# Attention and ternary feed-forward on one core: rows of x loaded interleaved, a step's queries turned by one transfer

## The chip, the cores and the metric

One core of one Trainium2 chip. The metric is device time of one launch in microseconds. The kernel before took 1701.72 us (median of 3 runs, 1698.91 to 1708.31). Engines are named as in the profile: PE (TensorE; PEld is its weight load), DVE (VectorE), ACT (ScalarE), POOL (GpSimd), SP (SyncE, which here only issues DMAs).

## The reference

```python
x = L0_attn_x                                   # [4, 1024, 512] f32
xn = layernorm(x)
c_Q  = rms_norm(xn @ Wq_down, q_norm_w)         # 512 -> 192
q_nop, q_pe = c_Q @ Wq_up, c_Q @ Wq_pe          # 16 heads x 128, 16 heads x 64
c_KV = rms_norm(xn @ Wkv_down, kv_norm_w)       # 512 -> 128
k_nop, v = split(c_KV @ Wkv_up)                 # 8 key/value heads x 128
k_pe = rms_norm(xn @ Wk_pe, k_pe_norm_w)        # one rotary key of 64 for all heads
q = concat(q_nop, rope(q_pe)); k = concat(k_nop, rope(k_pe))
attn = softmax(causal(q @ k.T * 192 ** -0.5))
y = (attn @ v) @ Wo
ffn = ternary(xn) @ (ternary(weight) + rram_variation).T
out = x + y + ffn
```

## The kernel before

**Latent form.** The prologue folds the key and value up-projections into the query and output weights, so that all 16 heads share one key matrix (128 latent numbers and 64 rotary ones a token, the rotary part held twice) and one value matrix of 128 numbers. Each fp32 number is held as a high and a low fp16 part, and a product is three matmuls (high by high, high by low, low by high).

**Tiles and steps.** A tile is 128 rows of x: 4 batches of 8 tiles, 32 in all, in the order of `ORDER`. The first three tiles of a batch are laid between the wide ones of the batch before. A tile has four steps, one for each group of four heads, so 128 steps `n`. Tile i of a batch sees i + 1 key blocks. A step has four score rows-of-128 `u = 4n + h`. With `a, g = divmod(h, 2)`, one of them holds 64 queries (side `a` of the tile) of two heads (pair `g`): the side with the first 64 queries needs 64 key columns fewer (`columns`).

**Queries.** PE makes a step's queries in PSUM with rows of x on the partitions (`up`, `up_pe`), ACT and DVE write high and low parts to `QS`, [128 rows, 1536]. SP then turns them by DMA (`turn_queries` in `sync_attention`, L1823 to L1832): two transfers, one for partitions 0 to 63 and one for 64 to 127, each to 12 blocks of 64 columns of `Q`. So a side's two heads lie next to each other, and `query_weights` (L413) takes 128 neighbouring columns as the stationary operand of the score matmuls (L672 to L676, L692 to L705), whose moving operand is the key matrix `K`.

**Softmax.** DVE adds the mask and takes the row's extreme (L1485), ACT the exponential and its sum (L1082), POOL scales the sum (L1719), DVE takes the reciprocal (L1493), ACT and DVE write the scaled high and low parts to `F` (L1077, L1499). SP turns `F` to `FT` by DMA (L1848).

**Values and output.** PE multiplies `V` (stationary) by `FT` (moving) into one PSUM bank of 512 columns (`weighed`, L724; matmuls L737 to L739, for the diagonal block of most steps L748 to L760 on halves, in the last step L774 to L776). The bank's columns are (head, side, query in the side), with the 64 queries of a side next to each other. ACT and DVE split the bank to `YH` and `YL`, and `combine` (L779) multiplies them as stationary operands by the output weights.

**Per tile.** `keep` (L1768) turns the tile's latents (`C`) and keys (`K`, L1784) by DMA and copies the values (`V`, L1786). The keys go straight to the tile's 128 columns of `K`.

**Order.** Each engine's program is written out by hand in one loop over steps. Scores of step n + 2 stand beside the values of step n on PE (`AHEAD = 2`), queries are made four steps ahead. SP's queue holds, a step, the turning of queries of step n + 3 and that of `F` of step n + 2, and once a tile `turn_x` and `keep`, all in program order.

Of the kernel before, what the change touches and what calls it, by code (L numbers as in the profile page):

```python
# [15 lines left out]
T = NB * NT  # L16
# [168 lines left out]
def rows(dram, t):  # L185

    b, i = ORDER[t]
    return dram[b, i * 128:i * 128 + 128, :]

# [13 lines left out]
class Memory:  # L203


    def __init__(self, ctx, nc):
# [37 lines left out]
        self.FT = own("FT", [128, RING * 1024], F16)  # L244
        self.Q = own("Q", [128, 2, 2, 768], F16)
        self.QS = own("QS", [128, 2, 1536], F16)
# [78 lines left out]
class Sems:  # L325


    def __init__(self, ctx, nc):
# [10 lines left out]
        self.ld_x, self.st_o, self.xt_in = sems("ld_x", XSLOTS), sem("st_o"), sem("xt_in")  # L339
        self.c_in, self.k_in, self.v_in = sem("c_in"), sem("k_in"), sem("v_in")  # L340
        self.const, self.wqs, self.nwq = sem("const"), sem("wqs"), sem("nwq")
# [18 lines left out]
        self.qh, self.ql, self.ph, self.pl = sem("qh"), sem("ql"), sem("ph"), sem("pl")  # L360
        self.q_in = [sems("q_first", 2), sems("q_second", 2)]
        self.s, self.mk, self.ex, self.sm, self.rc, self.fh, self.fl = (
# [50 lines left out]
def query_weights(m, n, h):  # L413


    a, g = divmod(h, 2)
    Q = m.Q[:, n % 2, a, :]
    return [Q[:, 256 * x + 128 * g:256 * x + 128 * g + 128] for x in range(3)]

# [225 lines left out]
def tensor_attention(e, m, s, tiles, queries):  # L645
# [12 lines left out]
    def score(n, h):  # L658
        b, i, g = where(n)
        u = 4 * n + h  # L660
        off, cuts = score_cuts(u)
        base = key_slot(b, 0) * 128
        qh, ql, qp = query_weights(m, n, h)
        e.wait_ge(s.q_in[h // 2][n % 2], 16 * (n // 2 + 1))
        e.wait_ge(s.k_in, 16 * (n // NG + 1))
        if u >= 2:
            e.wait_ge(s.mk, u - 1)
        else:
            e.wait_ge(s.wfl, 4)
        for lo, hi in cuts:  # L670
            o, keys = m.pS[u % 2][:, off + lo:off + hi], slice(base + lo, base + hi)
            e.eng.matmul(o, qh, m.K[:, AHI, keys], start=True, stop=False)  # L672
            e.eng.matmul(o, qh, m.K[:, ALO, keys], start=False, stop=False)
            e.eng.matmul(o, ql, m.K[:, AHI, keys], start=False, stop=False)
            e.eng.matmul(o, qp, m.K[:, BHI, keys], start=False, stop=False)
            op = e.eng.matmul(o, qp, m.K[:, BLO, keys], start=False, stop=True)  # L676
        op.then_inc(s.s, 1)

    def pair(n, p):
# [3 lines left out]
        base, K = key_slot(b, 0) * 128, m.K  # L683
        e.wait_ge(s.q_in[p][n % 2], 16 * (n // 2 + 1))
        e.wait_ge(s.k_in, 16 * (n // NG + 1))
        for h in (2 * p, 2 * p + 1):
# [24 lines left out]
    def weigh_ready(n):  # L711

        for z in range(GROUP_OF[4 * n], GROUP_OF[4 * n + 3] + 1):
            e.wait_ge(s.ft_in[z % FSLOTS], 16 * (z // FSLOTS + 1))
        e.wait_ge(s.v_in, 16 * (n // NG + 1))
        if n >= 2:
# [7 lines left out]
    def weighed(n, j, lo, hi):  # L724


        b, i, g = where(n)
        ft = turned_at(m, n, 0, 1024 * (i + 1)).rearrange("p (h c q) -> p h c q", h=4, q=128)
        V = m.V[:, key_slot(b, j), :, :]
        o = m.pY[n % 2].rearrange("p (h a q) -> p a h q", h=4, a=2)[:, lo // 2:hi // 2]  # L730
        return o, V[:, 0, :], V[:, 1, :], by_sides(ft[:, lo:hi, j, :]), by_sides(ft[:, lo:hi, i + 1 + j, :])
# [31 lines left out]
    def weigh_pair(p):  # L763
# [6 lines left out]
        ft = turned_at(m, n, 0, 1024 * (i + 1)).rearrange("p (h c q) -> p h c q", h=4, q=128)[:, p::2, :, :]  # L770
        o = m.pY[(n + p) % 2][:, 0:256].rearrange("p (h a q) -> p a h q", h=2, a=2)
        for j in range(i + 1):
# [84 lines left out]
class ScalarTiles:  # L857
# [63 lines left out]
    def parts_hi(self, t):  # L921
# [3 lines left out]
        if t:  # L925
            e.wait_ge(s.c_in, 16 * t)
            e.wait_ge(s.k_in, 16 * t)
            e.wait_ge(s.v_in, 16 * t)
        self.copy(m.CC[:, 0, 0, 0:192], m.CR[:, 0:192], m.RM[:, 4, 0:1])
# [3 lines left out]
class ScalarQueries:  # L933
# [5 lines left out]
    def queries_hi(self, n):  # L939
        e, m, s = self.e, self.m, self.s  # L940
        e.wait_ge(s.up, n + 1)
        if n >= 2:
            e.wait_ge(s.q_in[0][n % 2], 16 * (n // 2))
            e.wait_ge(s.q_in[1][n % 2], 16 * (n // 2))
        e.eng.activation(m.QS[:, n % 2, 0:512], m.pU, ACT.Copy).then_inc(s.qh, 1)  # L945

    def rotated_hi(self, n):
        e, m, s = self.e, self.m, self.s
        e.wait_ge(s.ropea, n + 1)
        if n >= 2:  # L950
            e.wait_ge(s.q_in[0][n % 2], 16 * (n // 2))
            e.wait_ge(s.q_in[1][n % 2], 16 * (n // 2))
        e.eng.activation(rotated_parts(m, n)[0], m.R1.rearrange("p (g h) d -> p g h d", g=2), ACT.Copy).then_inc(s.ph, 1)  # L953
# [121 lines left out]
def scalar_attention(e, m, s, A, out, tiles, queries):  # L1075
# [41 lines left out]
    def store_half(k):  # L1117
# [4 lines left out]
        at = slice(256 * k, 256 * k + 256)  # L1122
        e.eng.dma_start(rows(out, T - 1)[:, at], m.X[:, (T - 1) % XSLOTS, at]).then_inc(s.st_o, 16)

# [63 lines left out]
class VectorTiles:  # L1188
# [63 lines left out]
    def parts_lo(self, t):  # L1252
# [4 lines left out]
        if t:  # L1257
            e.wait_ge(s.kl, t)
            e.wait_ge(s.c_in, 16 * t)
            e.wait_ge(s.k_in, 16 * t)  # L1260
            e.wait_ge(s.v_in, 16 * t)
        e.eng.scalar_tensor_tensor(out=m.KR[:, 0, :], in0=m.CR[:, 320:384], scalar=r[2], in1=m.nwk[:, :],
# [212 lines left out]
def vector_attention(e, m, s, tiles, queries):  # L1475
# [61 lines left out]
    e.wait_ge(s.sco, 1)  # L1537
    e.wait_ge(s.ld_rope, 48)
    e.wait_ge(s.const, 10)
# [80 lines left out]
class PoolTiles:  # L1620
# [10 lines left out]
    def rotate_keys(self, t):  # L1631
        e, m, s = self.e, self.m, self.s
        i = ORDER[t][1]
        e.wait_ge(s.ld_rope, 48)
        e.wait_ge(s.k0, t + 1)
# [7 lines left out]
    def keys(self, t):  # L1643
# [28 lines left out]
def gpsimd_prologue(e, m, s, A, tiles, queries, outputs):  # L1672
# [24 lines left out]
    e.eng.tensor_scalar(m.tern[:, :, :], m.fw[:, :, :], -0.2, None, ALU.is_lt).then_inc(s.tern, 1)  # L1697
    e.wait_ge(s.v_in, 16)
    outputs.load(2)
# [10 lines left out]
    e.wait_ge(s.fm, 1)  # L1710
    e.eng.memset(m.mask[:, 0:256], 0.0).then_inc(s.zero, 1)


def gpsimd_attention(e, m, s, tiles, queries):
# [9 lines left out]
    for n in range(N):  # L1724
        t, g = divmod(n, NG)
        for p in range(2):
# [14 lines left out]
            if (g, p) == (1, 1) and t + LEAD < T:  # L1741
                tiles.x_lo(t + LEAD)

class SyncTiles:
# [20 lines left out]
    def keep(self, t):  # L1768
# [6 lines left out]
        if t >= 2:  # L1775
            e.wait_ge(s.up, NG * (t - 1))
        if b:
            e.wait_ge(s.wom, 16)
        if b >= 2:
            e.wait_ge(s.s, 4 * NG * (LAST_OF[b - 2] + 1))  # L1780
            e.wait_ge(s.pv, JBASE[NG * (LAST_OF[b - 2] + 1)])
        e.eng.dma_start_transpose(out=m.C[:, t % 2, :, :], in_=m.CC[:, 0, :, :].rearrange("p a n -> p (a n)")).then_inc(
            s.c_in, 16)
        e.eng.dma_start_transpose(out=m.K[:, :, at * 128:at * 128 + 128],  # L1784
                                  in_=m.CC[:, 1, :, :].rearrange("p a n -> p (a n)")).then_inc(s.k_in, 16)
        e.eng.dma_start(m.V[:, at, :, :], m.CC[:, 1, :, 0:128]).then_inc(s.v_in, 16)  # L1786

# [13 lines left out]
def sync_prologue(e, m, s, A, tiles, outputs):  # L1801
# [7 lines left out]
    load_x(1)  # L1809
    e.eng.dma_start(m.rope[:, :, :, :], A["rope"].rearrange("(n p) a d -> p n a d", p=128)).then_inc(s.ld_rope, 16)  # L1810
    e.eng.dma_start(m.mask[0:64, 960:1024], A["mask"][0:64, 0:64]).then_inc(s.ld_rope, 16)
# [142 lines left out]
```

## Time and profile before

| | |
|---|---|
| median of 3 runs | 1701.72 us |
| profiled execution, and its span | 1702.12 us, 1700.3 us |
| PE busy | 1633.8 us (96%), 9612 matmuls |
| DVE, ACT, POOL busy | 1301.6 (77%), 1104.3 (65%), 580.3 us (34%) |
| DMA queue q1 (SP's), share of 16 DMA engines | 80.3% |
| chain that ended last: PE, DMA | 71%, 9% |

The profile is of one execution. A matmul's duration contains its way through the array, and neighbours overlap, so the distance from one start to the next is what it occupies of PE. A weight load overlaps the matmul before it. A DMA transpose costs the queue of SP the time to issue it (its duration in a timeline) and lands later.

### The profile page before, as it was taken

Reading aid. Unit: us, or ns where it says so; the run is one execution under the profiler, and the core shown is the slowest. Engines: PE = TensorE matmul, PEld = TensorE weight load, DVE = VectorE, ACT = ScalarE, POOL = GpSimd, SP = SyncE. Lnnn points to the kernel's source line nnn. Section 1 sums busy time; section 2 is a strip of 40 time slices with the busy share of each in tenths; the row PEclk is TensorE's granted clock in tenths of the full one; section 3 lists DMA queues with packets and bytes.
Section 4 is the critical chain, followed back from the end, with each engine's and each line's share of the span. In section 5 each row is a group of like instructions: output and inputs, shape, how many; then the busy total and the mean of one; then the engine's idle time right before and its main releaser. Section 6 shows DMA issues by size and latency. Waiting matters only on the chain.

```text
span 1700.3 us, 30407 instructions
## 1 busy us (share of the span) xinstructions
PE 1633.8 (96%) x9612; PEld 837.1 (49%) x9612; DVE 1301.6 (77%) x3369; ACT 1104.3 (65%) x2464; POOL 580.3 (34%) x1048
## 2 busy tenths in 40 slices
PE   4789999999999999999999999999999999999999
PEld 3445455544544445545454445554455444555444
DVE  5888878768688687777868787876868868777765
ACT  5877667567576666656666566756756666666663
POOL 3323334333343233433333333433333323333320
PEclk9999999999999999999999999999999999999999
DMA  9467988879979889987969988887987988998886
GB/s 259 97 103 141 150 147 154 147 134 158 152 138 161 145 152 159 166 149 122 161 126 167 170 148 147 154 149 129 161 153 141 159 144 151 162 159 147 147 153 126
DMA packets 914889, 254.58 MB, mean 150 GB/s; under 512 B 901608, under 2 KB 904042, under 8 KB 914410
## 3 DMA queue, kind: packets, MB, share of 16 engines
q1 hardware_dynamic: 904032, 228.98, 80.3%
q10 hardware_dynamic: 9162, 17.37, 3.3%
q0 software_dynamic: 1536, 6.29, 1.1%
q8 instruction: 77, 1.26, 0.3%
q14 instruction: 82, 0.67, 0.1%
HBM read 19.76 MB, written 8.39 MB: 17 GB/s over the span
## 4 chain that ended last, share of the span: by engine, by line
PE 71%; DMA 9%; issue 6%; ACT 5%; DVE 5%; SPq 2%; POOL 2%; ACTq 0%; DVEq 0%; POOLq 0%
DMA FT<-F 6%; PE bank L695 5%; PE bank L693 5%; PE bank L692 5%; PE bank L694 5%; PE bank L795 5%; PE bank L794 5%; PE bank L793 5%; PE bank L737 4%; PE bank L738 4%; PE bank L739 4%; PE bank L705 4%; ACT P L1082 2%; SPq L1848 2%; DVE F L1499 2%
## 5 line engine op out<-in xcount | busy, mean ns | idle before, releaser
L1082 ACT ACTIVATE P<-P,nm 128x256 f32<-128x256 f32 (+15 forms) x512 | 381.7, 746 | 439.6 <-DVE nm L1485 439.6
L1485 DVE CUSTOM_DVE_ANT_0 P<-bank,mask,neg 128x256 f32<-128x256 f32 (+15 forms) x512 | 383.0, 783 | 270.0 <-PE bank L705 261.8
L1719 POOL TENSOR_SCALAR sn<-sm 128x1 f32<-128x1 f32 x512 | 209.0, 409 | 926.1 <-ACT P L1082 918.6
L1077 ACT ACTIVATE F<-P,rc 128x256 f16<-128x256 f32 (+15 forms) x512 | 366.7, 743 | 101.0 <-DVE rc L1493 62.4
L1499 DVE SCALAR_TENSOR_TENSOR F<-P,rc,F 128x256 f16<-128x256 f32 (+15 forms) x512 | 401.6, 796 | 2.7 <-ACT F L1077 2.3
L692 PE MATMUL bank<-K,Q 128*128 128x512 f16 (+7 forms) x760 | 241.7, 319 | 0.8 <-DMA Q<-QS 0.8
L695 PE MATMUL bank<-K,Q 128*128 128x512 f16 (+7 forms) x760 | 241.7, 319 | 0.0
L693 PE MATMUL bank<-K,Q 128*128 128x512 f16 (+7 forms) x760 | 241.7, 319 | 0.0
L694 PE MATMUL bank<-K,Q 128*128 128x512 f16 (+7 forms) x760 | 241.7, 319 | 0.0
L793 PE MATMUL bank<-WO,YH 128*128 128x512 f16 x512 | 194.3, 379 | 4.0 <-DVE YL L1505 3.7
L794 PE MATMUL bank<-WO,YH 128*128 128x512 f16 x512 | 194.0, 379 | 0.0
L795 PE MATMUL bank<-WO,YL 128*128 128x512 f16 x512 | 194.0, 379 | 0.0
L737 PE MATMUL bank<-FT,V 128*128 128x512 f16 x444 | 168.3, 379 | 11.2 <-DMA FT<-F 11.2
L1663 POOL TENSOR_TENSOR R<-R,R 128x256 f32<-128x256 f32 x128 | 146.3, 1143 | 68.0 <-DVE R L1298 67.8
L739 PE MATMUL bank<-FT,V 128*128 128x512 f16 x444 | 168.3, 379 | 0.0
L738 PE MATMUL bank<-FT,V 128*128 128x512 f16 x444 | 168.3, 379 | 0.0
L1303 DVE TENSOR_TENSOR QS<-bank,QS 128x512 f16<-128x512 f32 x128 | 87.3, 682 | 29.1 <-ACT QS L945 28.8
L692 PEld LDWEIGHTS bank<-K,Q 128*128 128x128 f16 x760 | 74.3, 98 | 69.4 <-issue 2.5
L693 PEld LDWEIGHTS bank<-K,Q 128*128 128x128 f16 x760 | 74.4, 98 | 66.1 <-issue 0.3
L1669 POOL TENSOR_TENSOR QS<-R,QS 128x256 f16<-128x256 f32 x128 | 101.8, 795 | 10.9 <-ACT QS L953 5.8
L1493 DVE RECIPROCAL rc<-sn 128x1 f32<-128x1 f32 x512 | 75.2, 157 | 39.1 <-POOL sn L1719 20.2
L695 PEld LDWEIGHTS bank<-K,Q 128*128 128x128 f16 x760 | 74.4, 98 | 48.2
(229 smaller groups left out, 2874.8 us busy)
## 6 DMA issues: line engine op xcount, KB each, us to landing
out<-X ACTq DMA_DIRECT2D x31, 256.0 KB, 3.6
X<-in_x ACTq DMA_DIRECT2D x28, 256.0 KB, 3.5
FT<-F SPq DMA_TRANSPOSE x348, 4.4
wo<-in_Wo POOLq DMA_DIRECT2D x4, 1024.0 KB, 7.0
Q<-QS SPq DMA_TRANSPOSE x256, 3.6
V<-CC SPq DMA_DIRECT2D x32, 64.0 KB, 3.0
X<-in_x SPq DMA_DIRECT2D x4, 256.0 KB, 8.4
kv<-in_Wkv_up POOLq DMA_DIRECT2D x1, 1024.0 KB, 12.5
```

The costliest lines, as they stand in the source:

```text
L692: e.eng.matmul(o, qh, K[:, AHI, keys], start=True, stop=False)
L693: e.eng.matmul(o, qh, K[:, ALO, keys], start=False, stop=False)
L694: e.eng.matmul(o, ql, K[:, AHI, keys], start=False, stop=False)
L695: e.eng.matmul(o, qp, K[:, BHI, keys], start=False, stop=False)
L737: e.eng.matmul(o, vh, hi, start=start, stop=False)
L793: e.eng.matmul(m.pO, yh, wh, start=(g == 0 and h == 0), stop=False)
L794: e.eng.matmul(m.pO, yh, wl, start=False, stop=False)
L795: op = e.eng.matmul(m.pO, yl, wh, start=False, stop=(g == NG - 1 and h == 3))
L1077: return e.eng.activation(dst, src, ACT.Copy, scale=scale)
L1082: e.eng.activation(m.P[:, u % 4, 0:w], m.P[:, u % 4, 0:w], ACT.Exp, bias=m.nm[:, u % 8:u % 8 + 1], scale=-1.0, accum_out=m.sm[:, u % 8:u % ...
L1485: e.eng.tensor_tensor_reduce(out=m.P[:, u % 4, 0:w], in0=m.pS[u % 2][:, off:off + w], in1=m.mask[:, end - w:end], scale=m.neg[:, :], scala ...
L1499: e.eng.scalar_tensor_tensor(out=m.F[:, slot, at + lo:at + lo + w], in0=m.P[:, u % 4, 0:w], scalar=m.rc[:, u % 8:u % 8 + 1], in1=m.F[:, sl ...
```

## The change

Rows of a tile are laid on the partitions alternately: partition 2k holds row k and partition 2k + 1 row 64 + k (`by_places`), on loading x and on storing the result. The rotary table is loaded in that order too, by two transfers in place of one. A side's queries are now the even or the odd partitions of `QS`, and the columns of same parity after turning. One transfer of all 128 partitions turns a step's queries (L1854 in the new kernel), and the stationary operand of the score matmuls is every second column of 256 (`[:, a::2]`). Keys come out of the DMA in the interleaved order, into a buffer `KT`, and POOL copies them to `K` in the order of rows (`keep_keys`, one copy of 128 x 512 a tile, with a semaphore `k_at` for which the scores now wait). Values are put in the order of rows by two transfers of 64 partitions. The product of values and probabilities is written to PSUM so that YH and YL keep the interleaved order: the bank's columns are now (head, query in the side, side), and a matmul writes every second column.

```diff
@@ -185,7 +185,13 @@
     b, i = ORDER[t]
-    return dram[b, i * 128:i * 128 + 128, :]
+    return by_places(dram[b, i * 128:i * 128 + 128, :])
+
+
+def by_places(dram):
+
+
+    return dram.rearrange("(a k) n -> k a n", a=2)
...
@@ -223,6 +229,7 @@
         self.K = own("K", [128, 4, 2048], F16)
+        self.KT = own("KT", [128, 4, 128], F16)
         self.V = own("V", [128, 2 * NT, 2, 128], F16)
...
@@ -242,7 +249,7 @@
         self.FT = own("FT", [128, RING * 1024], F16)
-        self.Q = own("Q", [128, 2, 2, 768], F16)
+        self.Q = own("Q", [128, 2, 12, 128], F16)
         self.QS = own("QS", [128, 2, 1536], F16)
...
@@ -337,7 +344,7 @@
         self.ld_x, self.st_o, self.xt_in = sems("ld_x", XSLOTS), sem("st_o"), sem("xt_in")
-        self.c_in, self.k_in, self.v_in = sem("c_in"), sem("k_in"), sem("v_in")
+        self.c_in, self.k_in, self.v_in, self.k_at = sem("c_in"), sem("k_in"), sem("v_in"), sem("k_at")
         self.const, self.wqs, self.nwq = sem("const"), sem("wqs"), sem("nwq")
...
@@ -358,7 +365,7 @@
         self.qh, self.ql, self.ph, self.pl = sem("qh"), sem("ql"), sem("ph"), sem("pl")
-        self.q_in = [sems("q_first", 2), sems("q_second", 2)]
+        self.q_in = sems("q_in", 2)
         self.s, self.mk, self.ex, self.sm, self.rc, self.fh, self.fl = (
...
@@ -414,8 +421,8 @@
     a, g = divmod(h, 2)
-    Q = m.Q[:, n % 2, a, :]
-    return [Q[:, 256 * x + 128 * g:256 * x + 128 * g + 128] for x in range(3)]
+    Q = m.Q[:, n % 2, :, :]
+    return [Q[:, 4 * x + 2 * g:4 * x + 2 * g + 2, :].rearrange("p h q -> p (h q)")[:, a::2] for x in range(3)]
...
@@ -661,8 +668,8 @@
         qh, ql, qp = query_weights(m, n, h)
-        e.wait_ge(s.q_in[h // 2][n % 2], 16 * (n // 2 + 1))
-        e.wait_ge(s.k_in, 16 * (n // NG + 1))
+        e.wait_ge(s.q_in[n % 2], 16 * (n // 2 + 1))
+        e.wait_ge(s.k_at, n // NG + 1)
         if u >= 2:
...
@@ -681,8 +688,8 @@
         base, K = key_slot(b, 0) * 128, m.K
-        e.wait_ge(s.q_in[p][n % 2], 16 * (n // 2 + 1))
-        e.wait_ge(s.k_in, 16 * (n // NG + 1))
+        e.wait_ge(s.q_in[n % 2], 16 * (n // 2 + 1))
+        e.wait_ge(s.k_at, n // NG + 1)
         for h in (2 * p, 2 * p + 1):
...
@@ -712,7 +719,7 @@
             e.wait_ge(s.ft_in[z % FSLOTS], 16 * (z // FSLOTS + 1))
-        e.wait_ge(s.v_in, 16 * (n // NG + 1))
+        e.wait_ge(s.v_in, 32 * (n // NG + 1))
         if n >= 2:
...
@@ -727,7 +734,7 @@
         V = m.V[:, key_slot(b, j), :, :]
-        o = m.pY[n % 2].rearrange("p (h a q) -> p a h q", h=4, a=2)[:, lo // 2:hi // 2]
+        o = m.pY[n % 2].rearrange("p (h q a) -> p a h q", h=4, a=2)[:, lo // 2:hi // 2]
         return o, V[:, 0, :], V[:, 1, :], by_sides(ft[:, lo:hi, j, :]), by_sides(ft[:, lo:hi, i + 1 + j, :])
...
@@ -768,7 +775,7 @@
         ft = turned_at(m, n, 0, 1024 * (i + 1)).rearrange("p (h c q) -> p h c q", h=4, q=128)[:, p::2, :, :]
-        o = m.pY[(n + p) % 2][:, 0:256].rearrange("p (h a q) -> p a h q", h=2, a=2)
+        o = m.pY[(n + p) % 2][:, 0:256].rearrange("p (h q a) -> p a h q", h=2, a=2)
         for j in range(i + 1):
...
@@ -925,7 +932,7 @@
             e.wait_ge(s.k_in, 16 * t)
-            e.wait_ge(s.v_in, 16 * t)
+            e.wait_ge(s.v_in, 32 * t)
         self.copy(m.CC[:, 0, 0, 0:192], m.CR[:, 0:192], m.RM[:, 4, 0:1])
...
@@ -940,16 +947,14 @@
         if n >= 2:
-            e.wait_ge(s.q_in[0][n % 2], 16 * (n // 2))
-            e.wait_ge(s.q_in[1][n % 2], 16 * (n // 2))
+            e.wait_ge(s.q_in[n % 2], 16 * (n // 2))
         e.eng.activation(m.QS[:, n % 2, 0:512], m.pU, ACT.Copy).then_inc(s.qh, 1)
...
         if n >= 2:
-            e.wait_ge(s.q_in[0][n % 2], 16 * (n // 2))
-            e.wait_ge(s.q_in[1][n % 2], 16 * (n // 2))
+            e.wait_ge(s.q_in[n % 2], 16 * (n // 2))
         e.eng.activation(rotated_parts(m, n)[0], m.R1.rearrange("p (g h) d -> p g h d", g=2), ACT.Copy).then_inc(s.ph, 1)
...
@@ -1631,7 +1636,7 @@
         i = ORDER[t][1]
-        e.wait_ge(s.ld_rope, 48)
+        e.wait_ge(s.ld_rope, 64)
         e.wait_ge(s.k0, t + 1)
...
@@ -1651,6 +1656,19 @@
         e.eng.tensor_tensor(lo, twice, hi, ALU.subtract).then_inc(s.kl, 1)
+
+
+    def keep_keys(self, t):
+        e, m, s = self.e, self.m, self.s
+        b, i = ORDER[t]
+        at = key_slot(b, i) * 128
+        e.wait_ge(s.k_in, 16 * (t + 1))
+        if b:
+            e.wait_ge(s.wom, 16)
+        if b >= 2:
+            e.wait_ge(s.s, 4 * NG * (LAST_OF[b - 2] + 1))
+        e.eng.tensor_copy(m.K[:, :, at:at + 128].rearrange("p c (a k) -> p c a k", a=2),
+                          m.KT.rearrange("p c (k a) -> p c a k", a=2)).then_inc(s.k_at, 1)
...
@@ -1695,7 +1713,8 @@
     e.eng.tensor_scalar(m.tern[:, :, :], m.fw[:, :, :], -0.2, None, ALU.is_lt).then_inc(s.tern, 1)
-    e.wait_ge(s.v_in, 16)
+    tiles.keep_keys(0)
+    e.wait_ge(s.v_in, 32)
     outputs.load(2)
...
@@ -1709,6 +1728,7 @@
     e.eng.memset(m.mask[:, 0:256], 0.0).then_inc(s.zero, 1)
+    tiles.keep_keys(1)
...
@@ -1740,6 +1760,8 @@
                 tiles.x_lo(t + LEAD)
+            if (g, p) == (3, 1) and t + LEAD - 1 < T:
+                tiles.keep_keys(t + LEAD - 1)
...
@@ -1774,16 +1796,17 @@
             e.wait_ge(s.up, NG * (t - 1))
+            e.wait_ge(s.k_at, t)
         if b:
...
         if b >= 2:
-            e.wait_ge(s.s, 4 * NG * (LAST_OF[b - 2] + 1))
             e.wait_ge(s.pv, JBASE[NG * (LAST_OF[b - 2] + 1)])
...
             s.c_in, 16)
-        e.eng.dma_start_transpose(out=m.K[:, :, at * 128:at * 128 + 128],
+        e.eng.dma_start_transpose(out=m.KT[:, :, :],
                                   in_=m.CC[:, 1, :, :].rearrange("p a n -> p (a n)")).then_inc(s.k_in, 16)
-        e.eng.dma_start(m.V[:, at, :, :], m.CC[:, 1, :, 0:128]).then_inc(s.v_in, 16)
+        for a in range(2):
+            e.eng.dma_start(m.V[64 * a:64 * a + 64, at, :, :], m.CC[a::2, 1, :, 0:128]).then_inc(s.v_in, 16)
...
@@ -1807,7 +1830,8 @@
     load_x(1)
-    e.eng.dma_start(m.rope[:, :, :, :], A["rope"].rearrange("(n p) a d -> p n a d", p=128)).then_inc(s.ld_rope, 16)
+    for a in range(2):
+        e.eng.dma_start(m.rope[a::2, :, :, :], A["rope"].rearrange("(n a k) x d -> a k n x d", a=2, k=64)[a]).then_inc(s.ld_rope, 16)
     e.eng.dma_start(m.mask[0:64, 960:1024], A["mask"][0:64, 0:64]).then_inc(s.ld_rope, 16)
...
@@ -1827,9 +1851,7 @@
             e.wait_ge(s.s, 4 * (n - 1))
-        for a in range(2):
-            e.eng.dma_start_transpose(out=m.Q[:, n % 2, a, :].rearrange("p (c q) -> p c q", q=64),
-                                      in_=m.QS[64 * a:64 * a + 64, n % 2, :]).then_inc(s.q_in[a][n % 2], 16)
+        e.eng.dma_start_transpose(out=m.Q[:, n % 2, :, :], in_=m.QS[:, n % 2, :]).then_inc(s.q_in[n % 2], 16)
```

The instructions of PE, DVE and ACT stand in the same order and have the same shapes as before. SP's and POOL's differ at the places below.

SP, the end of the narrow tile (1, 0) and the first transfers of probabilities of the wide tile (0, 6) after it: `Q<-QS` is the turning of queries, `FT<-F` that of probabilities, `K` and `V` belong to `keep`. The kernel before:

```order
105 L1831 DMA_TRANSPOSE Q<-QS 128x12x64 x2
106 L1848 DMA_TRANSPOSE FT<-F 128x8x128
107 L1762 DMA_TRANSPOSE XT<-XS 128x12x128
108 L1782 DMA_TRANSPOSE C<-CC 128x4x128
109 L1784 DMA_TRANSPOSE K<-CC 128x4x128
110 L1786 DMA V<-CC 128x2x128
111 L1848 DMA_TRANSPOSE FT<-F 128x14x128 x2
```

The kernel after, at the same place of SP's queue:

```order
105 L1854 DMA_TRANSPOSE Q<-QS 128x12x128
106 L1870 DMA_TRANSPOSE FT<-F 128x8x128
107 L1784 DMA_TRANSPOSE XT<-XS 128x12x128
108 L1804 DMA_TRANSPOSE C<-CC 128x4x128
109 L1806 DMA_TRANSPOSE KT<-CC 128x4x128
110 L1809 DMA V<-CC 64x2x128 x2
111 L1870 DMA_TRANSPOSE FT<-F 128x14x128 x2
```

Two transposes of queries became one of the same bytes, the keys go to `KT`, and the values take two transfers. Nothing else moved on SP.

POOL, the last step of tile 0, where `sn<-sm` scales a sum of the softmax, `R` and `QS` are the queries' rotary parts. The kernel before:

```order
71 L1719 TENSOR_SCALAR sn<-sm 128x1 x2
72 L1669 TENSOR_TENSOR QS<-R_75,QS 128x2x2x64
73 L1719 TENSOR_SCALAR sn<-sm 128x1 x2
74 L1663 TENSOR_TENSOR R_75<-R_75,R_76 128x256
75 L1719 TENSOR_SCALAR sn<-sm 128x1 x2
```

The kernel after, at that place:

```order
73 L1739 TENSOR_SCALAR sn<-sm 128x1 x2
74 L1687 TENSOR_TENSOR QS<-R_76,QS 128x2x2x64
75 L1670 COPY K<-KT 128x4x128
76 L1739 TENSOR_SCALAR sn<-sm 128x1 x2
77 L1681 TENSOR_TENSOR R_76<-R_76,R_77 128x256
```

The copy of the keys stands behind the queries' low part in the fourth step of each tile, ahead of the next step's sums.

## Rows read from the trace of the kernel before

**Rows 1.** The page: PE's busy time, and three lines by slice.

```profile
PE 1633.8 (96%) x9612; PEld 837.1 (49%) x9612; DVE 1301.6 (77%) x3369; ACT 1104.3 (65%) x2464; POOL 580.3 (34%) x1048
...
PE   4789999999999999999999999999999999999999
...
PEclk9999999999999999999999999999999999999999
DMA  9467988879979889987969988887987988998886
```

**Rows 2.** The page: SP's DMA queue.

```profile
q1 hardware_dynamic: 904032, 228.98, 80.3%
```

**Rows 3.** Waits of PE: who waited for whom, us in total, times, longest.

```profile
PE bank L737 <- DMA FT<-F: 11.2, 11, 1.7
...
PE bank L748 <- DMA FT<-F: 4.2, 6, 1.2
...
PE bank L692 <- DMA Q<-QS: 0.8, 1, 0.8
```

**Rows 4.** Timeline of SP's queue, 343 to 358 us: start, us, what.

```profile
342.44 3.39 SPq L1831 DMA_TRANSPOSE Q<-QS  x2
345.93 4.71 SPq L1848 DMA_TRANSPOSE FT<-F  x2
...
355.67 0.60 SPq L1786 DMA_DIRECT2D V<-CC  x1
```

**Rows 5.** Timeline of PE at 354 us.

```profile
354.44 0.38 PE L737 MATMUL bank<-FT,V 128*128 128x512 f16 x1 [1.71 <-DMA FT<-F]
354.65 0.38 PE L738 MATMUL bank<-FT,V 128*128 128x512 f16 x1
```

**Rows 6.** Lines L1831 and L1762 by themselves: duration ns min/median/max on SP's queue.

```profile
L1831 SPq DMA_TRANSPOSE Q<-QS x256: 1217/1488/2662, 53.1 to 1652.0; - x128
...
L1762 SPq DMA_TRANSPOSE XT<-XS x31: 1273/1713/3302, 47.7 to 1504.8; - x31
```

**Rows 7.** Groups by shape, PE, products of values: busy us, mean ns.

```profile
L737 PE MATMUL bank<-FT,V 128*128 128x512 f16 x444 | 168.3, 379 | 11.2 <-DMA FT<-F 11.2
...
L757 PE MATMUL bank<-FT,V 128*128 128x256 f16 x124 | 35.1, 283 | 0.0
```

**Rows 8.** Groups by shape, PE, scores of narrow width.

```profile
L692 PE MATMUL bank<-K,Q 128*128 128x192 f16 x88 | 21.6, 246 | 0.0
...
L705 PE MATMUL bank<-K,Q 64*128 64x256 f16 x96 | 13.2, 272 | 0.0
...
L705 PE MATMUL bank<-K,Q 64*128 64x192 f16 x64 | 7.9, 243 | 0.0
L692 PE MATMUL bank<-K,Q 128*128 128x128 f16 x32 | 7.0, 219 | 0.8 <-DMA Q<-QS 0.8
...
L692 PE MATMUL bank<-K,Q 128*128 128x64 f16 x24 | 4.1, 193 | 0.0
```

**Rows 9.** Timeline of PE at 340 us: score matmuls of 64 columns.

```profile
340.04 0.19 PE L692 MATMUL bank<-K,Q 128*128 128x64 f16 x1
...
340.30 0.19 PE L697 MATMUL bank<-K,Q 128*128 128x64 f16 x1
```

**Rows 10.** Groups by shape, PEld: weight loads in f16 and f32.

```profile
L692 PEld LDWEIGHTS bank<-K,Q 128*128 128x128 f16 x760 | 74.3, 98 | 69.4 <-issue 2.5 <-DMA Q<-QS 1.3
...
L585 PEld LDWEIGHTS bank<-tk,tq 128*128 128x128 f32 x64 | 9.3, 226 | 1.8 <-ACT tq L864 1.3 <-DVE WM L1334 0.2
```

**Rows 11.** Timeline of PE in the prologue: matmuls in f32.

```profile
31.33 0.60 PE L555 MATMUL bank<-ident,kv 128*128 128x128 f32 x4
31.77 1.95 PE L585 MATMUL bank<-tk,tq 128*128 128x128 f32 x16
```

**Rows 12.** Groups by shape, POOL: a copy of 128 columns, an operation on 512.

```profile
L1629 POOL TENSOR_TENSOR XS<-XN,XS 128x512 f16<-128x512 f32 x32 | 37.1, 1160 | 62.3 <-ACT XS L864 62.3
...
L1651 POOL COPY CC<-CC 128x128 f16<-128x128 f16 x32 | 9.5, 296 | 0.0
```

More of the change, by code:

```diff
@@ L1122, in store_half @@
         at = slice(256 * k, 256 * k + 256)
-        e.eng.dma_start(rows(out, T - 1)[:, at], m.X[:, (T - 1) % XSLOTS, at]).then_inc(s.st_o, 16)
+        e.eng.dma_start(rows(out, T - 1)[:, :, at], m.X[:, (T - 1) % XSLOTS, at]).then_inc(s.st_o, 16)
     def outputs_out(o):
@@ L1260, in parts_lo @@
             e.wait_ge(s.k_in, 16 * t)
-            e.wait_ge(s.v_in, 16 * t)
+            e.wait_ge(s.v_in, 32 * t)
         e.eng.scalar_tensor_tensor(out=m.KR[:, 0, :], in0=m.CR[:, 320:384], scalar=r[2], in1=m.nwk[:, :],
@@ L1633, in rotate_keys @@
         i = ORDER[t][1]
-        e.wait_ge(s.ld_rope, 48)
+        e.wait_ge(s.ld_rope, 64)
         e.wait_ge(s.k0, t + 1)
```

## The prediction

> **What bounds the kernel now.** I read the page's busy times first, then its lines by slice, then the waits of PE, then SP's queue, then single shapes. PE is busy 1633.8 of 1700.3 us, and by slice it is below nine tenths only in the first three of 40 slices, the prologue; the granted clock is in the top tenth in every slice, so at the upper of its two levels, 2.4 GHz, [rows 1]. "Busy" can hide idle streaming, so I looked at distances from start to start: a values matmul of 512 columns starts 0.21 us after the one before [rows 5], which is 512 columns at 2.4 GHz (213 ns) and nothing else. Ten score matmuls of 64 columns, each with a weight load of its own, lie between 340.04 and 340.30 us, so about 29 ns each for 27 ns of streaming [rows 9]. PE streams without a gap. Any column that gets slower is paid in full, and what can be won back is only its waits. Those are 11.2 us in 11 places on L737 and 4.2 us in 6 places on L748, both on the turned probabilities, and 0.8 us once on the turned queries [rows 3].
>
> DMA is the second resource: SP's queue takes 80.3% of 16 engines' time [rows 2], eight or nine tenths in most slices [rows 1]. The place where it reaches PE is seen at 354 us: SP spends 342.44 to 345.83 us on the pair of query transposes, 345.93 to 350.64 us on the two `FT<-F` directly behind [rows 4], and PE stands 1.71 us for an FT until 354.44 us [rows 5]. SP had no pause between the two, so the pair's length sets when the probabilities leave.
>
> **Query transfers, the gain.** One transpose of 128 partitions and 12 blocks takes the place of two of 64 partitions, 128 times. The pair costs SP 2 x 1.488 = 2.98 us by the median, 2 x 1.217 = 2.43 us at least. The turning of x has just the new shape, 128 partitions by 12 blocks, and costs 1.713 us by the median and 1.273 us at least [rows 6]. So a step's SP time falls by about 1.27 us (1.16 us by the minima). Over 128 steps that is 160 us of SP's time, nearly all of it off the path. On the path are the 17 places where PE waited for FT, together 15.4 us, 0.9 us each [rows 3]. A shift of 1.27 us would cover most of them whole, and the longest, 1.7 us, in part. But only where SP's queue, and not DVE or ACT with `F`, was last; and the data moved stay the same 254 bytes a packet (228.98 MB in 904032 packets) [rows 2], so where DMA engines rather than the issue are full, less comes back. I take two thirds, 10 us. Ends: 0, and 16 us (all 15.4 us and the 0.8 us for queries). What is late after that is the softmax chain itself, two steps ahead of its use.
>
> **Values in two transfers.** A second `V<-CC` costs SP 0.60 us a tile [rows 4], behind `keep`'s transposes and before the queries of a step three ahead. 32 x 0.60 = 19 us of SP time against 160 us saved: nothing on the path. If that cover fails it delays one FT a tile by 0.6 us less the 1.27 us saved, which is still a gain.
>
> **Keys by POOL.** A copy of 128 x 128 in f16 took 296 ns, an operation of 512 columns with two inputs 1160 ns [rows 12]. A copy of 512 columns with a source step of two lies between these; nearer the upper row by its size, so I take 0.9 us. Added up it is 32 x 0.9 = 29 us on an engine that is busy 34% of the span [rows 1]. Behind the copy on POOL stand the two sums of the next step, so a softmax row can come 0.9 us later once a tile. That row is used two steps later on PE, so it costs nothing but where PE waits for FT anyway. The new wait, for the keys' DMA, is met: `keep` stands in the third step, the copy in the fourth, and the keys are first used two steps after that. In the prologue the first copy stands before two loads of Wo and can shift them by a microsecond. I take 1 us for all of this. Ends: 0, and 8 us (a quarter of 32 x 0.9).
>
> **Score weights with a step of two.** The loads are hidden beneath the matmul before: 98 ns of a load of 128 columns in f16, while 64 columns of matmul came every 29 ns [rows 9, 10]. So loads now run far faster one behind the other than their 98 ns tell, and there is room. No row has a load with a step. The nearest is the load in f32, whose columns are also 4 bytes apart: 226 ns [rows 10], and f32 matmuls of 128 columns start 0.11 us apart (four in 31.33 to 31.77) [rows 11]. If a stepped load held PE to that 0.11 us, then 120 matmuls of 64 columns (24 on each of five lines) would lose 0.081, 132 of 128 columns (four lines of 32, and four of a fifth) 0.054, 376 of 192 columns (four lines of 88, and 24) 0.027 us, together 27 us; and 48 pairs of the halved matmul with 256 columns (two loads a pair, 0.22 less 0.11 us) and 32 pairs with 192 (0.22 less 0.08) 10 us [rows 8]. Ends: 0 and 37 us. I take 0, because a load of the same count of columns and the same type is nearer than one of another type, and the 29 ns show slack beneath all wider matmuls. The Trainium skill, "TensorE: Matmul & The Clock Gate", section on Fast Weight Load, says that the fast load is used for 128 columns that aren't fp32 with any step within about a thousand elements; by that rule the sum is the same 0, and no run here shows it yet.
>
> **Values written to every second column of PSUM.** Same count, same columns, but the destination has a step of two f32 numbers. No matmul of the trace writes so; runs of 64 neighbouring columns are the shortest it has. I take 0, because those broken runs already stream at 0.21 us for 512 [rows 5]. The other end is the rival below.
>
> **The sum.** Profiled execution 1702.1 us (span 1700.3 us and 1.8 us around it), minus 10, plus 1: 1693. It lies 0.4 us above the median of the runs shown, so against the median it is 1692.7; I say 1693. That is 0.5% below, right at what a measurement here can tell from no change (0.5%, 8.5 us), so faster and same share this case. Its own range is 1684 to 1701.
>
> **Rival 1: the stepped write halves the rate of the values matmuls (slower).** Place: L737 to L739 and the diagonal's L748 to L760. Mechanism: PE gives a column every 0.417 ns; if the accumulator's write takes neighbouring pairs together and stepped columns singly, a matmul takes twice its streaming. Price: 3 x 444 matmuls of 512 columns by 213 ns more are 284 us; six lines of 124 matmuls with 256 columns by 107 ns are 79 us [rows 7]; the last step adds 48 of 256 columns, 5 us. Sum 368 us, all of it exposed as PE has no slack, less some 15 us of waits that fall away: 1702 + 368 - 15 = 2055, range 2035 to 2075. It decides from a price of 0.005 us on each of those 2076 matmuls, which is already all the gain. For it: the engine runs so close to one column a cycle that any limit of the receiving side shows. Against it: reading and writing in runs of 64 is free. The Trainium skill, "Advanced Engine Details and Errata", section "Memory Cachelines", says that PSUM has lines of 8 bytes, two f32 values, and that "Every two consecutive elements should be contiguous for best throughput", and "PSUM — Partial Sum Buffer" (Specifications) repeats it; a step of two breaks just this. By this rule the time is that of this rival; the trace neither bears it out nor denies it.
>
> **Rival 2: the stepped weights show (slower).** The 37 us from above, less the 9 us: about 1730, range 1706 to 1740. For it: 628 score matmuls are no wider than 192 columns [rows 8]. Against: 29 ns apart with loads between [rows 9].
>
> **Rival 3: the transfers weren't the limit (same).** The bytes are as before and packets have 254 bytes in the mean [rows 2]; if the DMA engines and not SP's issue set when FT lands, or DVE's `F` is last at the 17 places, the gain is 0 to 4 us: about 1700.
>
> **How the numbers follow.** Forecast 0.50 (0.30 faster, 0.20 within 0.5%), rival 1 0.35, rival 2 0.08, rival 3 0.07. Faster 0.30, same 0.27, slower 0.43. The likeliest time is 1693. To leave out no more than 2 in 10 the range must reach rival 1, so 1684 to 2072; nothing is expected between 1740 and 2035.
>
> **What would show it.** Right: L737 to L739 and L757 with the mean of [rows 7] and starts 0.21 us apart; waits of PE for FT below 8 us in place of 15.4; SP's time for queries near 1.7 us a step; ten scores of 64 columns still within 0.26 us; a key copy of 0.9 us and no wait of PE for `K`. Rival 1: means of L737 to L739 near 0.6 us, starts 0.43 us apart, the share of DMA down to two thirds as all stretches. Rival 2: scores of 64 and 128 columns alone get further apart. The forecast is wrong if PE's waits stay at 15 us with shorter query transfers, or if any values matmul takes longer.

## The result: 2039 us, 20% slower

The kernel after takes 2039.3 us (median of 4 runs, 2038.08 to 2040.62), the kernel before 1701.7 us. The ratio is 1.198, 95% interval 1.194 to 1.201. The forecast was 1693. The time lies in the range of its first rival, 2055 with 2035 to 2075.

The page of the kernel after, the lines that answer to [rows 1] and [rows 2] (line numbers of the kernel after are 5 to 25 higher from here on, and each kernel of an experiment has its own):

```profile
span 2038.8 us, 30219 instructions
...
PE 1993.7 (98%) x9612; PEld 911.6 (45%) x9612; DVE 1309.9 (64%) x3369; ACT 1115.3 (55%) x2464; POOL 603.0 (30%) x1080
...
PEclk9999999999999999999999999999999999999999
...
q1 hardware_dynamic: 900464, 228.96, 63.3%
```

PE has the same 9612 matmuls, but 360 us more of busy time, at the same granted clock. DVE and ACT have the same number of instructions as before and 8 and 11 us more of busy time; POOL has the 32 key copies more, 19.8 of its 23 us more. The share of the DMA queue fell from 80.3% to 63.3%. Most of that is the longer span, as the kernel with the stepped write alone (below) has 65.3%; the rest is the new form of the transfers.

The kernel after, groups by shape of PE, to be read against [rows 7] and [rows 8]:

```profile
L745 PE MATMUL bank<-FT,V 128*128 128x512 f16 x444 | 281.5, 634 | 0.0
L746 PE MATMUL bank<-FT,V 128*128 128x512 f16 x444 | 281.5, 634 | 0.0
L744 PE MATMUL bank<-FT,V 128*128 128x512 f16 x444 | 275.0, 619 | 0.0
...
L764 PE MATMUL bank<-FT,V 128*128 128x256 f16 x124 | 48.3, 390 | 0.0
...
L699 PE MATMUL bank<-K,Q 128*128 128x192 f16 x88 | 21.6, 246 | 0.0
```

Two matmuls of the values after one another, from the timeline of PE (start us, us, what), against [rows 5]:

```profile
1000.44 0.63 PE L744 MATMUL bank<-FT,V 128*128 128x512 f16 x1
1000.87 0.63 PE L745 MATMUL bank<-FT,V 128*128 128x512 f16 x1
```

Values matmuls start 0.43 us apart in place of 0.21. Scores have the mean that they had, and ten of 64 columns with stepped weights lie as close as in [rows 9]:

```profile
395.14 0.19 PE L699 MATMUL bank<-K,Q 128*128 128x64 f16 x1
...
395.40 0.19 PE L704 MATMUL bank<-K,Q 128*128 128x64 f16 x1
```

So the score matmuls, whose weights have the step, lost nothing, and the values matmuls, whose write has it, take twice as long. On POOL, against [rows 12], the key copy:

```profile
L1670 POOL COPY K<-KT 128x512 f16<-128x512 f16 x32 | 19.8, 617 | 0.0
```

### The profile page after: what moved, and what is told of

Read it like the earlier page. It is cut to its first block, busy times and chain, and to the rows that moved or that the text cites. A ratio compares the mean times of both kernels' runs of the same rounds, so it can differ in the third digit from the quotient of the medians.

```text
span 2038.8 us, 30219 instructions
## 1 busy us (share of the span) xinstructions
PE 1993.7 (98%) x9612; PEld 911.6 (45%) x9612; DVE 1309.9 (64%) x3369; ACT 1115.3 (55%) x2464; POOL 603.0 (30%) x1080
## 3 DMA queue, kind: packets, MB, share of 16 engines
q1 hardware_dynamic: 900464, 228.96, 63.3%
## 4 chain that ended last, share of the span: by engine, by line
PE 94%; DVE 1%; DMA 1%; issue 1%; POOL 1%; ACT 1%; DVEq 0%; POOLq 0%; ACTq 0%; SPq 0%
PE bank L744 9%; PE bank L745 9%; PE bank L746 9%; PE bank L699 6%; PE bank L701 6%; PE bank L702 6%; PE bank L700 6%; PE bank L800 5%; PE bank L802 5%; PE bank L801 5%; PE bank L712 4%; PE bank L764 2%; PE bank L766 2%; PE bank L471 1%; PE bank L502 1%; PE bank L507 1%
## 5 line engine op out<-in xcount | busy, mean ns | idle before, releaser
L745 PE MATMUL bank<-FT,V 128*128 128x512 f16 x444 | 281.5, 634 | 0.0
L746 PE MATMUL bank<-FT,V 128*128 128x512 f16 x444 | 281.5, 634 | 0.0
L744 PE MATMUL bank<-FT,V 128*128 128x512 f16 x444 | 275.0, 619 | 0.0
L800 PE MATMUL bank<-WO,YH 128*128 128x512 f16 x512 | 198.7, 388 | 3.3 <-DVE YL L1510 3.2
L801 PE MATMUL bank<-WO,YH 128*128 128x512 f16 x512 | 194.0, 379 | 0.0
L746 PEld LDWEIGHTS bank<-FT,V 128*128 128x128 f16 x444 | 61.7, 139 | 128.8 <-issue 128.8
L951 ACT ACTIVATE QS<-bank 128x512 f16<-128x512 f32 x128 | 75.5, 590 | 74.5 <-PE bank L507 74.5
L1687 POOL TENSOR_TENSOR QS<-R,QS 128x256 f16<-128x256 f32 x128 | 101.7, 794 | 10.9 <-ACT QS L958 5.8
L700 PEld LDWEIGHTS bank<-K,Q 128*128 128x128 f16 x760 | 74.4, 98 | 67.0 <-issue 0.3
L699 PEld LDWEIGHTS bank<-K,Q 128*128 128x128 f16 x760 | 74.4, 98 | 66.8 <-issue 0.2
```

The source lines that it names most:

```text
L699: e.eng.matmul(o, qh, K[:, AHI, keys], start=True, stop=False)
L700: e.eng.matmul(o, qh, K[:, ALO, keys], start=False, stop=False)
L744: e.eng.matmul(o, vh, hi, start=start, stop=False)
L745: e.eng.matmul(o, vh, lo, start=False, stop=False)
L746: e.eng.matmul(o, vl, hi, start=False, stop=stop).then_inc(s.pv, 1)
L800: e.eng.matmul(m.pO, yh, wh, start=(g == 0 and h == 0), stop=False)
```

## The experiments

**One edit undone: the write, with ACT and DVE reading with a step.** The bank is now filled side after side, without a step. Taking the two sides alternately is left to those who empty it.

```diff
-        o = m.pY[n % 2].rearrange("p (h q a) -> p a h q", h=4, a=2)[:, lo // 2:hi // 2]
+        o = m.pY[n % 2].rearrange("p (a h q) -> p a h q", h=4, a=2)[:, lo // 2:hi // 2]
...
-        copy(m.YH[:, n % 2, :], m.pY[n % 2], 2.0 ** -4).then_inc(s.yh, 1)
+        copy(parts_of(m.YH[:, n % 2, :]), in_places(m.pY[n % 2]), 2.0 ** -4).then_inc(s.yh, 1)
...
+def in_places(bank):
+    return bank.rearrange("p (a k) -> p k a", a=2)
+def parts_of(part):
+    return part.rearrange("p (k a) -> p k a", a=2)
```

The reads of DVE for YL and those of the last step are changed likewise.

> The kernel after, but the values matmuls write their bank side by side (columns: side, head, query; each side's 256 columns without a step), and ACT and DVE read the bank with a step of 256 columns between the two sides, so that YH and YL are as in the kernel after. All else of the change stays: stepped weights, one query transfer, keys by POOL. Theory W (the stepped write to PSUM is the whole loss): L745 and its neighbours are back at a mean of 0.379 us and starts 0.216 us apart, and the time is 1693 (1684 to 1702), below the kernel before, as the forecast's gain now shows. Rival S (the loss comes from something else of the change: weights with a step, keys by POOL, the new waits): the time stays near 2039. Rival R (reading PSUM with a step costs ACT and DVE): 128 reads on each get longer, the YH copy above 0.58 us, and the time is above 1710.

Measured: 1692.07 us (1688.76 to 1692.86, 6 runs), ratio to the kernel before 0.9934 (0.9920 to 0.9948). Theory W holds, rival S falls: everything else of the change is in this kernel. The difference to the kernel after is 347 us. One group of PE and three waits of PE in this kernel:

```profile
L754 PE MATMUL bank<-FT,V 128*128 128x512 f16 x444 | 168.3, 379 | 2.4 <-DMA FT<-F 2.4
```

```profile
PE bank L467 <- DMA XT<-XS: 4.8, 5, 1.5
...
PE bank L754 <- DMA FT<-F: 2.4, 4, 1.0
...
PE bank L765 <- DMA FT<-F: 1.1, 2, 0.6
```

The waits for turned probabilities are 3.5 us in place of the 15.4 us of [rows 3]; those for `XT` are 4.8 us, in the kernel before 2.9 us. SP's queue in this kernel:

```profile
q1 hardware_dynamic: 900464, 228.96, 77.8%
```

That is 52 us less than before in the mean of the 16 engines (77.8% of 1687.9 us against 80.3% of 1700.3 us), with the same bytes.

Rival R falls too. The group of YH on ACT, in the kernel before and then in this one, and that of YL on DVE in this one:

```profile
L1077 ACT ACTIVATE YH<-bank 128x512 f16<-128x512 f32 x127 | 73.9, 582 | 2.8 <-PE bank L739 2.8
```

```profile
L1092 ACT ACTIVATE YH<-bank 128x512 f16<-128x512 f32 x127 | 73.9, 582 | 2.8 <-PE bank L756 2.8
L1520 DVE SCALAR_TENSOR_TENSOR YL<-bank,YH 128x512 f16<-128x512 f32 x127 | 86.5, 681 | 7.7 <-ACT YH L1092 7.7
```

DVE took 681 ns for YL in the kernel before as well. Reading PSUM in turn from two places 256 columns apart costs neither engine anything. This version is faster than both kernels.

**The same, but the step in the write of ACT and DVE.** The diff is against the version before.

```diff
-    return bank.rearrange("p (a k) -> p k a", a=2)
+    return bank.rearrange("p (a k) -> p a k", a=2)
...
-    return part.rearrange("p (k a) -> p k a", a=2)
+    return part.rearrange("p (k a) -> p a k", a=2)
```

> As e1_read_turned, but ACT and DVE read the bank in its order and write YH and YL (f16, SBUF) with a step of two elements. Theory W: 1693 (1684 to 1702), the same as e1 within 0.2%, as either step is hidden. If a stepped f16 write costs these engines (YH copy above 0.58 us), the later YL lengthens PE's waits at L800 and the time is 3 to 15 us above e1.

Measured: 1692.32 us (1688.89 to 1694.17, 6 runs), ratio 0.9935 (0.9919 to 0.9950). The group of YH in this kernel:

```profile
L1092 ACT ACTIVATE YH<-bank 128x512 f16<-128x512 f32 x127 | 93.2, 734 | 2.7 <-PE bank L756 2.7
```

The stepped f16 write costs ACT 152 ns on top of 582 and DVE 49 ns on top of 681 (YL took 730 ns), and the time doesn't show it: the expected 3 to 15 us above the version before didn't come, the two are the same. PE's waits for YL grew by 1 us, from 3.7 to 4.7. The step in the read is still the better choice, as it adds no work to either engine.

**One edit alone: the kernel before with the stepped write.** YH comes out in the interleaved order while x is still laid in the order of rows. The kernel leaves out the edits that would match them, so the attention part of a tile comes out in another order of rows than x, and the result is not that of the reference; the count of instructions and their shapes are those of the kernel before.

```diff
-        o = m.pY[n % 2].rearrange("p (h a q) -> p a h q", h=4, a=2)[:, lo // 2:hi // 2]
+        o = m.pY[n % 2].rearrange("p (h q a) -> p a h q", h=4, a=2)[:, lo // 2:hi // 2]
```

> The kernel before with one edit: the values matmuls write every second column. ACT and DVE read the bank as before, so the rows of a tile come out in another order. Theory W: 512 columns from start to start in 0.429 us in place of 0.216, the whole time 2035 to 2060, that is the loss of the kernel after without any other part of it, plus about 10 us, as the query transfers are still two. Rival S: 1702, nothing.

Measured: 2039.23 us (one run), to a tenth of a microsecond the time of the kernel after. That edit is the whole loss. I expected this kernel to be about 10 us slower than the kernel after, as its query transfers are still two. It isn't: neither kernel has a wait of PE for FT in its list of waits, so with these longer values matmuls a shorter query transfer has nothing to win. That the longer steps leave the DMA time enough is my reading, not tested by itself.

```profile
L738 PE MATMUL bank<-FT,V 128*128 128x512 f16 x444 | 281.5, 634 | 0.0
```

**The price of a step by itself.** Behind the end of the kernel before stand groups of 16 equal matmuls into an unused bank. One loop as an example:

```diff
+    for _ in range(16):
+        e.eng.matmul(bank[:, 0:512:2], wt[:, 0:128], mv[:, 0:256], start=True, stop=True)
```

> The kernel before with 16 groups of 16 matmuls put behind its end (they write an unused bank, and their sources are what lies in FT). Each group changes one operand's step. Start to start: contiguous destination of 256 columns 0.109 us; destination step 2: 0.216; 128 columns contiguous 0.056, with step 3 or 4: 0.107 each, if what counts is whether the neighbour is taken in the same write (theory of pairs), 0.16 and 0.21 if the cost grows with the step. Runs of 2 columns that start on an even column: 0.109 by the theory of pairs; runs of 2 that start on an odd column: 0.216 if pairs are aligned to 8 bytes, 0.109 if not; runs of 4: 0.109. Moving operand with a step of 2 and of 8 f16 elements: 0.109 to 0.12; of 16: up to 0.22; two sides alternately, far apart: 0.109 if reads are free, 0.2 or more if not. Weights of 128 columns under 32 columns of moving: 0.025 to 0.03 us contiguous; with a step of 2 the same if the fast load holds, 0.107 if not; with steps of 8 and 16 open.

The timeline of PE: each row is a group, and the distance to the next row's start is 16 matmuls. A row's own length contains the way of the last matmul through the array.

```profile
1692.71 1.92 PE L856 MATMUL bank<-FT 128*128 128x256 f16 x16 [0.97 <-DVE X L1561]
1694.47 3.62 PE L858 MATMUL bank<-FT 128*128 128x256 f16 x16
1697.88 1.10 PE L860 MATMUL bank<-FT 128*128 128x128 f16 x16
1698.81 1.91 PE L862 MATMUL bank<-FT 128*128 128x128 f16 x16
1700.52 1.95 PE L864 MATMUL bank<-FT 128*128 128x128 f16 x16
1702.26 1.95 PE L866 MATMUL bank<-FT 128*128 128x256 f16 x16
1704.05 3.62 PE L868 MATMUL bank<-FT 128*128 128x256 f16 x16
1707.46 1.95 PE L870 MATMUL bank<-FT 128*128 128x256 f16 x16
1709.25 1.98 PE L872 MATMUL bank<-FT 128*128 128x256 f16 x16
1711.07 7.39 PE L874 MATMUL bank<-FT 128*128 128x256 f16 x16
1718.28 7.54 PE L876 MATMUL bank<-FT 128*128 128x256 f16 x16
1725.64 4.07 PE L878 MATMUL bank<-FT 128*128 128x256 f16 x16
1729.55 0.55 PE L880 MATMUL bank<-FT 128*128 128x32 f16 x16
1729.95 0.55 PE L882 MATMUL bank<-FT 128*128 128x32 f16 x16
1730.35 1.15 PE L884 MATMUL bank<-FT 128*128 128x32 f16 x16
1731.35 1.15 PE L886 MATMUL bank<-FT 128*128 128x32 f16 x16
```

As medians from start to start, in this run:

| what has the step | columns | ns from start to start |
|---|---|---|
| destination, none (L856) | 256 | 109 |
| destination, 2 (L858) | 256 | 216 |
| destination, none (L860) | 128 | 56 |
| destination, 3 and 4 (L862, L864) | 128 | 109, 109 |
| destination, runs of 2 from even columns (L866) | 256 | 109 |
| destination, runs of 2 from odd columns (L868) | 256 | 216 |
| destination, runs of 4 (L870) | 256 | 109 |
| moving f16, 2, 8, 16 (L872, L874, L876) | 256 | 113, 451, 460 |
| moving f16, two runs 2048 columns apart in turn (L878) | 256 | 244 |
| weights, none, 2, 8, 16 (L880 to L886) | 32 | 25, 25, 62, 62 |

The price doesn't grow with the step: 2, 3 and 4 all double the time. What counts is whether two columns that follow each other fall into the same aligned pair of f32 numbers. A pair that is begun on an odd column is two halves of two pairs, and costs as much as single columns. Each of the destination numbers is what the theory of pairs expected. For the moving operand I expected 109 to 120 ns at a step of 8 and up to 220 at 16; both are far worse.

The granted clock was at 2.4 GHz up to 1715.3 us, in the middle of L874, then at 1.2 GHz to 1728.9 us, near the end of L878, and at 2.4 GHz again for the weights. Before it fell PE had never paused, but its last ten matmuls, those of L874, had started only every 451 ns. L874 kept 451 ns and L878 its 244 ns on both sides of a change of level, so the read sets these, not the clock. The 460 ns for a step of 16 were seen at 1.2 GHz alone.

> As bench_steps, 16 other groups of 16 matmuls behind the end of the kernel before. Destination: two of each aligned four columns named were free (runs of 2, even) and twice as long (odd). So by the theory of aligned pairs: an odd start of 256 contiguous columns 0.109 us (one more pair); runs of 3 out of 4, 384 columns: 192 pairs of which half hold one column, so 192 x 0.83 = 0.160 to 0.21 us (a cycle of 1.2 GHz a pair touched), against 0.162 us contiguous; runs of 64 as in the kernel before 0.216 for 512; neighbours in two halves of the bank in turn 0.43 for 512. Moving f16: step 2 took 0.113 us for 256 and step 8 0.451. If a line of 16 bytes must be hit twice: steps 3 to 5 near 0.113 to 0.2, step 7 near 0.4; runs of 2 far apart 0.2 to 0.25, of 4 and of 8 0.109 to 0.15. Weights: step 2 0.025, step 8 0.062; step 3, 4 and 6 between.

The timeline of PE of that run, the groups that decide (256 columns to L868, then twice 384, 256 and twice 512):

```profile
1696.12 1.92 PE L856 MATMUL bank<-FT 128*128 128x256 f16 x16 [0.97 <-DVE X L1562]
1697.88 2.92 PE L858 MATMUL bank<-FT 128*128 128x256 f16 x16
1700.63 3.79 PE L860 MATMUL bank<-FT 128*128 128x256 f16 x16
...
1715.12 3.65 PE L866 MATMUL bank<-FT 128*128 128x256 f16 x16
1718.60 2.15 PE L868 MATMUL bank<-FT 128*128 128x256 f16 x16
...
1724.03 3.63 PE L878 MATMUL bank<-FT 128*128 128x384 f16 x16
1727.48 2.78 PE L880 MATMUL bank<-FT 128*128 128x384 f16 x16
1730.10 1.92 PE L882 MATMUL bank<-FT 128*128 128x256 f16 x16
1731.86 3.62 PE L884 MATMUL bank<-FT 128*128 128x512 f16 x16
1735.31 7.03 PE L886 MATMUL bank<-FT 128*128 128x512 f16 x16
```

An odd start of a contiguous run costs next to nothing (L882, 110 ns against 109). The form of the kernel before, runs of 64, takes 216 ns (L884), two halves of a bank in turn 429 (L886). Runs of 3 out of 4 (L878) take 217 ns against 163 contiguous (L880): 128 runs touch 256 pairs, at 0.85 ns a pair. My count of 192 pairs was wrong, the price a pair right. Moving f16 with steps of 3, 4, 5 and 7 took 172, 227, 284 and 396 ns (L858, L860 and the rows left out); those of 4 and 5 are worse than the 113 to 200 that I expected.

Runs of 2 far apart (L866) can't be read from this run. The granted clock was at 1.2 GHz from 1712.3 to 1719.1 us, over the whole of L866, and its 217 ns are what 256 columns take at that level anyway: in L868 one start lay 213 ns after the one before while the clock was low. After the clock had risen, L868 with its runs of 4 took 110 ns, and runs of 8 took 109, so these cost nothing. Weights with steps of 3, 4 and 6 took 27, 33 and 47 ns.

**Where the 10 us come from: the same bytes in two issues.**

```diff
-        e.eng.dma_start_transpose(out=m.Q[:, n % 2, :, :], in_=m.QS[:, n % 2, :]).then_inc(s.q_in[n % 2], 16)
+        for x in range(2):
+            e.eng.dma_start_transpose(out=m.Q[:, n % 2, 6 * x:6 * x + 6, :],
+                                      in_=m.QS[:, n % 2, 768 * x:768 * x + 768]).then_inc(s.q_in[n % 2], 16)
```

> The kernel of e1_read_turned (1692.07 us), but a step's queries are again turned by two transfers, of all 128 partitions and six blocks of 128 each (the same bytes, as many issues as in the kernel before). Theory I (the gain of 10 us is SP's time for the second issue): SP's pair takes 2.5 to 3 us again, PE's waits on FT return to some 12 to 16 us from 3.5, and the time is 1698 to 1704. Rival B (the gain is that full 128 partition transfers move faster, the count doesn't matter): pair and single take the same, 1692.

Measured: 1701.71 us (1698.87 to 1706.86, 11 runs), ratio to the kernel before 0.9991 (0.9977 to 1.0005). The version with one issue had 0.9934 (0.9920 to 0.9948), so the gain is gone. Lines L1865 of this kernel and L1864 of the version with one transfer by themselves, duration min/median/max on SP's queue:

```profile
L1865 SPq DMA_TRANSPOSE Q<-QS x256: 1209/1290/2481, 52.3 to 1648.2; - x128
```

```profile
L1864 SPq DMA_TRANSPOSE Q<-QS x128: 1413/1658/3753, 53.0 to 1637.7; - x128
```

Two issues are 2.58 us, one is 1.66 us. Waits of PE with two:

```profile
PE bank L754 <- DMA FT<-F: 5.6, 5, 2.0
PE bank L765 <- DMA FT<-F: 5.2, 6, 1.2
```

That is 10.8 us against 3.5, a little under the 12 to 16 that I expected. And its queue:

```profile
q1 hardware_dynamic: 904560, 228.98, 77.7%
```

The share is that of one issue (77.8%), not the 80.3% of the kernel before. So transfers of all 128 partitions do keep the DMA engines busy for less time, but this brought nothing: the gain came with the single issue and went with the second. Rival B falls.

**Keys copied three times by POOL**, each copy behind the end of the one before.

```diff
+        for x in range(3):
+            if x:
+                e.wait_ge(s.k_at, 3 * t + x)
...
```

> The kernel of e1_read_turned, but POOL makes each tile's key copy three times, each after the one before has ended (0.62 us one, so 1.3 us more a tile, 42 us more of POOL in all). Theory: the copy is hidden, as PE has more than a step of slack and POOL idles: 1692 to 1694. Rival: the sums behind the copy carry it to PE, up to 31 x 1.3 = 40 us; then the one copy of the change costs a third of the difference.

Measured: 1691.75 us (1691.10 to 1694.29, 5 runs), ratio 0.9940 (0.9928 to 0.9953), the same as with one copy. POOL's group in this kernel:

```profile
L1683 POOL COPY K<-KT 128x512 f16<-128x512 f16 x96 | 59.3, 618 | 3.9
```

40 us more of copies on POOL didn't reach PE. The one copy of the change is free.

## Why the prediction was wrong

- **What bounds the kernel: right.** PE streams without a gap but for its waits. That is why a slower column is paid in full. (The mean packet that the prediction gives as 254 bytes is 253 by [rows 2]; nothing hangs on it.)
- **Values written to every second column: the step that failed.** "I take 0, because those broken runs already stream at 0.21 us for 512" took a row on runs of 64 columns as the nearest to runs of one. It could not tell them apart: a run of 64 has 32 whole pairs. The question was at which length of a run the price begins, and that row had nothing to say on it. The runs show 0.43 us in place of 0.21, and the whole loss with this edit alone.
- **Rival 1: right in mechanism and place, 6% too high in its price.** The 368 us stand against 347 us between the kernel after and the one with that write undone. From start to start L744 to L746 lost 271 us, where 284 were worked out, and the last step 5, as worked out. The diagonal's six lines lost 50 us where I had 79: the three with 64 partitions start some 3 ns after a matmul on the other 64, run beside it, and cost 20 us together. Another 26 us are lost by the matmuls beside and behind them, those of `up_half` and `up_pe_half` and the first of `up` and `up_pe`, and 4 us are won at the scores. So the rival, too, had the place of some 26 us wrong. Its 15 us for waits were right: the kernel after has no wait for FT at all.
- **The rule of the Trainium skill** ("Advanced Engine Details and Errata", section "Memory Cachelines") that every two consecutive elements in PSUM should be contiguous agrees with these traces: aligned pairs are free, single columns take twice the time. The same section and the row that the prediction names in "PSUM — Partial Sum Buffer" (Specifications) say more widely that any non-contiguous pattern slows matmuls; that the runs deny, as runs of 64, of 4 and of an aligned 2 took the time of contiguous columns. I gave the rival 0.35 as no row bore on it. The kernel had no slack on the engine that the rule speaks of, and the price was worked out at 37 times the gain: even at 0.35 it was the larger stake.
- **Query transfers: right, where the stepped write is undone.** 10 us were taken, 15.4 us of waits became 3.5, and the version without the stepped write gained 10.9 us on the kernel before in the same runs (1702.95 to 1692.07). SP's time for a step's queries is 1.66 us by the median, 1.32 us less than the pair of the kernel before and 0.92 less than the pair of the version with two issues; I had 1.27. In the kernel after the shorter transfer is worth nothing, as the kernel with the stepped write alone takes the same time.
- **Rival 3: fell.** The bytes were not the limit: two issues of the same bytes lose the gain, with the same share of the DMA engines' time.
- **Weights with a step, rival 2: 0, right.** 25 ns at steps of 1 and 2.
- **Keys by POOL: right that it is hidden.** The copy took 0.617 us, I had 0.9, and three copies in place of one cost nothing, so the 1 us of the sum is not there. (A quarter of 32 x 0.9 us, the upper end, is 7 us and not 8.)
- **Values in two transfers: 0, not tested alone.** The runs show only that the kernel with this and all other edits but the stepped write comes out at the forecast.
- **The sum without the failed step** was 1693; measured 1692.07. So close a meeting is in part luck: the share of two thirds that was taken from the waits was a choice.

## What to carry to other kernels

Give a matmul a destination in which columns come in aligned pairs, and put a step that can't be avoided into the read of the engine that empties PSUM: on ACT and DVE the read cost nothing here. When a layout moves, write down for each operand of PE (weights, moving, destination) the length of its contiguous run before and after, as they have different prices, and don't let a row with a longer run stand for a shorter one. When SP's queue is the last thing before a wait, the count of issues matters though the bytes stay the same.

## What the runs showed of the hardware

- Destination of a matmul in PSUM: 0.84 to 0.88 ns for each aligned pair of f32 columns touched, whether one or both are written, at a granted clock of 2.4 GHz. So single columns take 216 ns for 256 against 109 for pairs.
- Moving operand in f16: 113 ns for 256 columns with a step of 2, 172 with 3, 227 with 4, 284 with 5, 396 with 7 and 451 with 8. An estimate from these: some 9 bytes are passed over a nanosecond for each partition. A step of 16 took 460 ns, at 1.2 GHz.
- The granted clock fell from 2.4 to 1.2 GHz with PE never idle, in groups whose matmuls started 396 and 451 ns apart for 256 columns (steps of 7 and 8).
- Weights of 128 columns under 32 moving ones: 25 ns for the matmul with its load up to a step of 2, 33 at 4, 62 at 8 and 16.
- ACT reading f32 from PSUM in turn from two places 256 columns apart: 582 ns as without, DVE 681 as without. Writing f16 to SBUF with a step of two: 734 and 730.
- A DMA transpose of 128 partitions and 12 blocks took 1.66 us of SP's queue, two of 6 blocks 2.58 us.
